# Routed scatters of the third and fourth batch: each waits for the one two places before it

## The reference

```
x = layernorm(x + lstm(x, w, u, bias))            # S = 8 groups, N = 512 tokens, D = 128
logits = x @ router_w;  top-2 experts, gates       # per token
dispatch to slot (group, expert, place), 128 slots per expert and group
h = gelu(xd @ w0[e]) * (xd @ w1[e]);  y = h @ wo[e]      # hidden size 680
out = layernorm(x + sum of gate * y over the two experts)
```

## Time and profile before

| what | value |
|---|---|
| median of 3 runs | 341.16 us (339.85 to 343.18) |
| profiled execution, its own time | 338.06 us |
| its span, first to last instruction | 335.9 us |
| busy: PE, DVE, ACT, POOL | 85%, 75%, 65%, 55% |
| granted TensorE clock, mean | 0.93 |
| scatters (line 511) | 64, 66.3 us busy |
| adds (line 526) | 60, 97.6 us busy |

### The profile page before, as it was taken

One profiled execution on the slowest core, in us unless ns is written; L12 is line 12 of the kernel. 1 busy time (PEld: TensorE's weight loads), 2 busy tenths in 40 slices (PEclk: granted clock), 3 DMA queues, 4 the chain that ended last, 5 costly groups with the idle time before them and its releaser, 6 DMA issues.

```text
span 335.9 us, 5632 instructions
## 1 busy us (share of the span) xinstructions
PE 287.1 (85%) x1676; PEld 240.0 (71%) x1676; DVE 251.5 (75%) x805; ACT 217.8 (65%) x498; POOL 186.3 (55%) x154
## 2 busy tenths in 40 slices
PE   8999999968622996329999999999999999999990
PEld 5666665658611886229999987877888888889890
DVE  2799989987501894027888889989877777999985
ACT  4687987877421573026777876876765666669884
POOL 5015888788775027787864444347347337368700
PEclk9999999998985699557999999999999999999996
DMA  7996294478751005334444336264324224523664
GB/s 226 361 406 191 68 239 138 131 153 247 168 179 47 19 27 150 104 36 46 50 65 58 51 49 176 50 145 57 48 22 56 34 23 86 114 22 40 95 187 132
DMA packets 46828, 37.74 MB, mean 112 GB/s; under 512 B 7073, under 2 KB 40800, under 8 KB 46800
## 3 DMA queue, kind: packets, MB, share of 16 engines
q1 hardware_dynamic: 35392, 26.56, 26.8%
q0 software_dynamic: 11408, 10.85, 21.0%
HBM read 17.86 MB, written 17.10 MB: 104 GB/s over the span
## 4 chain that ended last, share of the span: by engine, by line
PE 71%; DVE 13%; issue 7%; another core or an unknown queue 5%; ACT 3%; ACTq 0%; POOL 0%; DVEq 0%; POOLq 0%
PE big L676 12%; PE big L674 12%; PE big L675 11%; PE big L582 5%; PE b_xnt L690 3%; PE b_xnt L693 3%; PE b_xnt L691 3%; PE b_ht L693 3%; PE b_ht L690 2%; PE b_ht L691 2%; PE b_rt L710 2%; PE b_xt L626 2%; PE big L568 1%; PE b_ht L631 1%
## 5 line engine op out<-in xcount | busy, mean ns | idle before, releaser
L878 ACT ACTIVATE act_g<-big 128x256 f32<-128x256 f32 (+1 forms) x144 | 65.4, 454 | 88.9 <-PE big L676 57.6
L674 PE MATMUL big<-x_hi,e_hi 128*128 128x256 f32 (+1 forms) x264 | 88.8, 336 | 4.1 <-issue 3.8
L675 PE MATMUL big<-x_hi,e_lo 128*128 128x256 f32 (+1 forms) x264 | 86.0, 326 | 0.0
L676 PE MATMUL big<-x_lo,e_hi 128*128 128x256 f32 (+1 forms) x264 | 86.0, 326 | 0.0
L511 POOL DMA_INDIRECT slots<-rows,slot_ix x64 | 66.3, 1035 | 35.5 <-issue 18.6
L526 POOL DMA_INDIRECT tokens<-contrib,token_ix x32 | 52.0, 1625 | 38.6 <-DVE token_ix L1169 30.6
L526 POOL DMA_INDIRECT tokens<-zero_rows,token_ix x28 | 45.6, 1629 | 32.9 <-DVE token_ix L1169 25.8
L674 PEld LDWEIGHTS big<-x_hi,e_hi 128*128 128x128 f32 x264 | 52.0, 197 | 8.0 <-issue 3.5
L676 PEld LDWEIGHTS big<-x_lo,e_hi 128*128 128x128 f32 x264 | 51.7, 196 | 4.0
L675 PEld LDWEIGHTS big<-x_hi,e_lo 128*128 128x128 f32 x264 | 52.0, 197 | 3.4
L1177 DVE TENSOR_TENSOR h<-act_g,big 128x256 f32<-128x256 f32 (+3 forms) x36 | 18.3, 509 | 18.8 <-ACT act_g L878 13.7
(11 more groups left out here) (212 smaller groups left out, 683.9 us busy)
## 6 DMA issues: line engine op xcount, KB each, us to landing
e_raw<-in_L_ffn_w_kernel_dram SPq DMA_DIRECT2D x16, 320.0 KB
slots<-zero_rows SPq DMA_DIRECT2D x8, 548.0 KB, 8.1
e_lo<-e_raw POOLq DMA_DIRECT2D x5, 544.0 KB
e_raw<-in_L_ffn_wo_kernel_dram SPq DMA_DIRECT2D x8, 320.0 KB
xd<-slots SPq DMA_DIRECT2D x16, 137.0 KB
xd<-slots SPq DMA_DIRECT2D x8, 274.0 KB
x<-in_L_attn_input_seq_dram SPq DMA_DIRECT2D x8, 256.0 KB, 4.6
tokens<-rows SPq DMA_DIRECT2D x8, 256.0 KB
```

Source lines behind the costliest of these rows:

```text
L674: pe.matmul(dst, e_hi[q][:, c0:c0 + m], xdt_hi[u % 2][:, 0:w], start=True, stop=False)
L675: pe.matmul(dst, e_lo[q][:, c0:c0 + m], xdt_hi[u % 2][:, 0:w], start=False, stop=False)
L676: mm = pe.matmul(dst, e_hi[q][:, c0:c0 + m], xdt_lo[u % 2][:, 0:w], start=False, stop=True)
L878: nc.scalar.activation(act0[n % RH][0:m, 0:w], pre(n, P)[0], ACT.Gelu_apprx_tanh).then_inc(gelu_ready, 1)
```

## The change

The semaphore of a batch becomes two, one for each choice c. In the third and fourth batch a scatter of tile t > 0 first waits until all the earlier scatters of its own choice in the batch have landed. Since the choices alternate, that is the scatter two places before. SP waits for both semaphores of a batch in place of one. Nothing else is moved: the low copies and powers stand where they stood.

```
-        routed = [sem(f"routed{b}") for b in range(NB)]
+        routed = [[sem(f"routed{b}_{c}") for c in range(2)] for b in range(NB)]
...
             def load_xd(u):
                 r, gs = u % 4, groups(u)
                 for b in sorted({g // GB for g in gs}):
-                    sp.wait_ge(routed[b], 16 * 2 * BT)
+                    for c in range(2):
+                        sp.wait_ge(routed[b][c], 16 * BT)
...
                     for c in range(2):
+                        if b >= NB // 2 and t:
+                            pool.wait_ge(routed[b][c], 16 * t)
                         pool.indirect_dma_start(
                             slots, bass.IndirectOffsetOnAxis(ap=slot_ix[b][:, 2 * t + c:2 * t + c + 1], axis=0),
-                            rows[:, b * BT + t, :], None, bounds_check=slot_bound, oob_is_err=False).then_inc(routed[b], 16)
+                            rows[:, b * BT + t, :], None, bounds_check=slot_bound, oob_is_err=False).then_inc(routed[b][c], 16)
```

## The result

| | median | runs |
|---|---|---|
| before | 340.5 us (339.66 to 343.18) | 4 |
| after | 325.49 us (322.33 to 325.79) | 4 |
| ratio | 0.9525 (0.9444 to 0.9606) | |

The change takes 15 us off, outside my range (331 to 347) and on the side of rival one. The profiled execution of the kernel after took 325.79 us (span 324.0, granted clock 0.958).

The account below looks back on a forecast made before the run. The prediction saw PE as the bound (71% of the chain), with 29.0 us of standstill in two slow stages. Its certain terms summed to 0 on the median, so 341.2 us, range 331 to 347.

Parts of the forecast that it names:

- rival one: Third and fourth batch: pauses at the waits break PE's standstill; 331 to 337.5 us, both stages 324.5; chance 0.33.
- Where the loss is: PE at 93.0 to 109.3 and 131.8 to 151.8 us: 29.0 us of standstill, the kernel's largest loss.
- The two stages: PE's slow stretches, 93.0 to 109.3 and 131.8 to 151.8 us, with 18 and 31 matmuls; 13.6 and 15.4 us lost.
- Standstill as before: The forecast itself: both slow PE stages stay and the shift is hidden; 339 to 343.5 us, chance 0.42.
- the broken scatters before 79 us: Second batch's scatters, broken up by powers and low copies; PE starts 100 matmuls in 17.0 us beside them.
- How often the waits bind: Only beside weight loads: near 92.5 us in the third batch and 132 in the fourth, shifting them 2.0 and 1.5 us.
- my bounds of 5.5 and 5.0: Largest shifts of the third and fourth batch's scatters, with waits not free (3.5 us more each); the lower bound was 0.
- Waits free when met: On GpSimd a met wait was taken to cost 0; the other end was 3.5 us a batch.
- Landing in about 2.1 us at a quiet time: Scatter issue to seen landing, under two issue periods (2.57 us), so at quiet times the wait never binds.
- How late the semaphores are: PE's semaphore rise for the gelu at 148.85 us was put over 8 us after its matmul's recorded start.
- The shift is hidden: GpSimd's 16.57 us idle covers the third batch's shift, later waits for DVE the fourth's; certain sum 0.
- Rival two: Waits only lengthen the scatter trains while PE is slow: 2.8 us more, 344.0, up to 349.6 us; chance 0.25.

Follow-up runs that it names:

- the first comparison: Unchanged kernel at 302.47 us beside limits of one (341.13 us) and four (302.66 us) scatters under way, long pauses (302.41 us) and short pauses (302.91 us).
- the fifth and sixth: Unchanged kernel at 340.81 and 338.37 us; beside it long pauses (315.87 us) and held weight loads (338.96 us), then short pauses (328.98 us).

## Why the prediction was wrong, by its own steps

**Where the loss is: right.** The two stages were the largest loss that this change could touch. By the same measure their 29.0 us fell to 10.8, by 18 us, yet the span is only 11.9 us shorter. The rate was the error: by 175 us the kernel after has started 904 matmuls and before 801, and 103 matmuls at the 8.0 to 8.7 a microsecond of the undisturbed stages are 11.8 to 12.9 us.

**"Standstill as before", at 0.42: wrong, and this is the step that failed.** Its ground was that at a quiet time at most two scatters are in flight already, "that the change does next to nothing". I had set the cure at nothing because the queue is short. In its place the runs showed that the pauses at the waits break the standstill: 88 and 83 matmuls in the two stages in place of 18 and 31, 15 us. The run with long pauses and no waits on scatters takes off 24.9 us, so what cures is the pause in the issue; the run with the weight loads held keeps 14.3 us of lateness with at most two scatters in flight, so the number in flight is not what makes them late. I had the evidence for it in hand, the broken scatters before 79 us with 5.9 matmuls a microsecond, and gave it 0.33 because the pauses would be short.

**How often the waits bind: mis-sized.** I worked out one pause of 2.3 us in the third batch and two of 0.8 and 1.1 in the fourth. Measured were 0.87, 1.50, 1.29 and 1.12 us, and 0.51, 0.47, 1.20, 1.80 and 0.69. The places near the weight loads were right (here the loads are issued at 91.43 and 124.59 us); the 1.12 us before 104.33 has no load beside it. The shift is 4.3 and 3.3 us, inside my bounds of 5.5 and 5.0, about twice the values taken. More pauses, spread over each train, may also be why the change cures more than one pause would have by my working of rival one; no run separates that.

**Waits free when met: right.** 0.30 us before most scatters, as with none.

**Landing in about 2.1 us at a quiet time: nearly right.** With one under way the next is issued 2.60 us after the last; less the 0.30 us that stands between issues anyway that is 2.3 us. The Trainium skill ("DMA: Bandwidth & Descriptors", section "Anatomy of one DMA — SWDGE (gpsimd) path") gives 2.2 us by its fit, an estimate; the runs agree at quiet times, and those beside the weight loads don't.

**How late the semaphores are: read too low.** I set the gelu at 148.85 us against the matmul of 140.23, over 8 us. Counted off, the product that it waits for ended at 134.49 us, 14.4 us before.

**The shift is hidden: right here, with the bound now known.** SP's waits of the kernel after, 56 to 180 us, have no scatter among the long ones, as in the earlier trace rows:

```profile
SPq L437 <- DVE token_ix L1172: 49.8, 6, 14.6
```

Where no standstill is, the change costs 0.2 to 0.4% (ratios 1.0024, 1.0036 and 1.0019, against 1.003 for the kernel before itself), so next to nothing. The cover is thinner there, though: SP's wait for the rows of a batch, from 85 to 200 us, is 5.9 us in before and 11.5 and 12.8 in two profiles of the change. Slow each scatter by 1.3 us, and the cover ends: 18.7 us for one batch, 38.7 for both.

**Rival one: right in mechanism, and its own figure nearly exact, in part by luck.** "Both make 324.5": measured 325.49. Its premise that PE slows only after 9 us of train was wrong: the lateness starts 2.7 us into the fourth batch. The range stopped at 331, "short of both stages being cured", though nothing in the working spoke for one stage alone. And errors cancel: my 16.7 us for both stages went by the low rate, and the profiled execution gained 12.3 (338.06 to 325.79), where the medians lie 15.0 apart. **Rival two: refuted.** PE does not pay for the train's length: the kernel with long pauses has trains 7.1 us longer and is the fastest. The Trainium skill's rule in "DMA: Bandwidth & Descriptors", section "Rules for kernel authors", to issue early and wait late, did not decide here; it does where at most one is under way.

**What stays open.** The same kernel takes 302 or 340 us from one comparison to another, and nothing in its own work differs. It isn't tied to the chip: the first comparison, without the standstill, and the fifth and sixth, with it, ran on a chip of the same number. No run switches it. In the executions with standstill the trace holds 4,230 to 4,418 rises of semaphores, in the others 6,041 to 6,303; most of those lacking are rises made by DMAs (2,481 in before, 4,009 in the same kernel at 302 us). Whether the records are fewer because rises are held back, or whether the recording has a part in it, isn't shown. Wherever I looked at the lateness a train of scatters or adds stands beside it, but a train isn't enough. Nor is it shown what moves in steps of 0.71 us. The waits in one batch alone, which would split the gain, were run only where there was nothing to gain.

## What to carry to other kernels

When an engine is let go by "remote" well after its supposed releaser has ended, look at what GpSimd issues at that time: where semaphores come late beside an unbroken train of software-queue DMAs, short pieces of other work on GpSimd (1.1 us after every four scatters) took 24.9 of 340.8 us off, and cost nothing measurable where they don't (302.0 to 303.0 us beside 302.2 to 302.9). Try that before a limit on the number in flight, whose price is a landing of 2.3 us once it always binds. And a rival whose cure is already to be seen in the profile deserves its full figure in the range, however small the cause looks.

## What was not expected of the hardware

- PE's semaphores rose up to 16 us after the work that raises them, in steps near 0.71 us beside scatters and 0.05 us apart in most of the pauses.
- One kernel's median lay at 302 to 303 us in four comparisons and at 338 to 341 us in the result and two more, with runs of one comparison within about 1.6%.
- The granted clock followed the standstill, not the reverse. In before PE is busy for 0.3 of the 3 us from 93 to 96, while the clock is granted in full (2.4 GHz) until 97.7; from there to 114.8 it is at half (1.2 GHz). From 131 to 133 us PE is idle, and the clock is at half from 135.3 to 155.8. The means are 0.65 and 0.59 in the slow stages of before, 0.99 and 1.00 in the same stages at 302 us.
